# Expert rows scaled by their gates and added to token rows in DRAM by indirect transfers, in place of stores and gathers

## What is computed

```python
x = x + _L0_ffn_ref(_layernorm(x, axis=-1)[None], router_w, router_b, expert_w, expert_b)[0]
...
probs = jax.nn.softmax(logits, axis=-1)
top2_vals, top2_idx = jax.lax.top_k(probs, 2)
cw = cw.at[jnp.arange(n)[:, None], top2_idx].set(top2_vals)
h = jax.nn.gelu(jnp.einsum('nd,edh->neh', xf, W1) + b1[None], approximate=False)
y = jnp.einsum('neh,ehd->ned', h, W2) + b2[None]
out = jnp.einsum('ne,ned->nd', cw, y)
```

## Time and profile before

| | us |
|---|---|
| median of 3 runs (2142.50 to 2151.97) | 2149.12 |
| the profiled execution, its own time | 2141.64 |
| its span, first to last instruction | 2139.8 |
| TensorE matmuls busy | 1928.0 (90%) |
| VectorE busy | 757.1 (35%) |
| ScalarE busy | 397.3 (19%) |
| Pool busy | 132.0 (6%) |

### The profile page before, as it was taken

The page is one execution under the profiler, slowest core; times in us unless marked ns, Lnnn a source line. Parts: engine busy times, 40 slices in busy tenths (PEclk is TensorE's granted clock), DMA queues, the critical chain, the costliest instruction groups (busy, mean ns, idle before and its releaser), DMA issues.

```text
span 2139.8 us, 23079 instructions
## 1 busy us (share of the span) xinstructions
PE 1928.0 (90%) x7603; PEld 1234.0 (58%) x7604; DVE 757.1 (35%) x1715; ACT 397.3 (19%) x1046; POOL 132.0 (6%) x223
## 2 busy tenths in 40 slices
PE   5999999998999999779995999999999999399990
PEld 3555566566433446646663875555578589266560
DVE  3211322676688879411112511141111133311113
ACT  2331210024211112100100332000221211111110
POOL 0000000000000000011112300000000000111114
PEclk9999999999999999579997999999999999599995
DMA  6004000000000101424554410110010012434537
GB/s 174 0 1 155 2 0 1 19 1 0 20 29 28 42 21 44 162 74 176 188 180 131 139 59 0 44 45 0 0 45 1 0 59 61 159 125 170 183 118 223
DMA packets 58416, 154.05 MB, mean 72 GB/s; under 512 B 12574, under 2 KB 23218, under 8 KB 57893
## 3 DMA queue, kind: packets, MB, share of 16 engines
q1 hardware_dynamic: 34053, 87.05, 11.6%
q0 software_dynamic: 13200, 36.25, 5.5%
q10 hardware_dynamic: 11088, 29.77, 3.8%
HBM read 121.76 MB, written 34.78 MB: 73 GB/s over the span
## 4 chain that ended last, share of the span: by engine, by line
PE 86%; DMA 5%; DVE 4%; issue 2%; ACT 1%; DVEq 1%; POOL 1%; POOLq 0%; ACTq 0%; SPq 0%
PE PS L605 22%; PE PS L821 11%; PE PS L906 10%; PE PS L615 7%; PE PS L753 5%; PE PS L996 4%; PE PS L932 4%; PE PS L1016 4%; PE PS L669 4%; PE PS L973 3%; PE PS L959 3%; DMA WS<-in_fW 2%; DMA YG<-expert_rows,IDXA 2%; PE PS L884 1%; PE PS L803 1%
## 5 line engine op out<-in xcount | busy, mean ns | idle before, releaser
L605 PE MATMUL PS<-WS,XT 128*125 128x384 f32 x960 | 312.5, 487 | 1.4 <-issue 1.4
L821 PE MATMUL PS<-WR,F 125*65 125x500 f32 (+1 forms) x720 | 262.2, 518 | 2.5 <-DVE WR L1572 2.5
L605 PEld LDWEIGHTS PS<-WS,XT 128*125 128x125 f32 x960 | 180.0, 188 | 129.0 <-issue 2.6
L1572 DVE SCALAR_TENSOR_TENSOR WR<-RB,U,AT 125x500 f32<-125x500 f32 (+1 forms) x360 | 212.5, 647 | 22.0 <-PE PS L821 13.7
L906 PE MATMUL PS<-WS,XGT 128*128 x624 | 208.0, 490 | 0.0
L821 PEld LDWEIGHTS PS<-WR,F 125*65 125x65 f32 x720 | 97.6, 139 | 142.8 <-issue 99.8
L906 PEld LDWEIGHTS PS<-WS,XGT 128*128 128x128 f32 x624 | 117.7, 192 | 77.3 <-issue 2.5
L615 PE MATMUL PS<-XT,WS 128*128 128x416 f32 (+1 forms) x432 | 151.2, 512 | 0.0
L1698 DVE TENSOR_TENSOR YS<-PS,EBB 128x768 f32<-128x768 f32 x50 | 47.9, 958 | 270.5 <-PE PS L906 209.6
L615 PEld LDWEIGHTS PS<-XT,WS 128*128 128x128 f32 x432 | 81.6, 189 | 69.2 <-issue 69.2
L753 PE MATMUL PS<-OHS,OHD 125*125 125x418 bf16 x564 | 110.8, 351 | 0.0
(11 more groups left out here) (263 smaller groups left out, 1968.8 us busy)
## 6 DMA issues: line engine op xcount, KB each, us to landing
expert_rows<-YS ACTq DMA_DIRECT2D x50, 384.0 KB
WS<-in_ewT SPq DMA_DIRECT2D x8, 2304.0 KB, 10.6
WS<-in_fW SPq DMA_DIRECT2D x16, 1152.0 KB, 7.8
WS<-in_w SPq DMA_DIRECT2D x5, 2304.0 KB, 9.8
xn_rows<-XN ACTq DMA_DIRECT2D x20, 336.0 KB
RB<-expert_rows SPq DMA_DIRECT2D x12, 488.3 KB
WS<-in_wp SPq DMA_DIRECT2D x2, 2304.0 KB, 11.8
WS<-in_W SPq DMA_DIRECT2D x2, 2304.0 KB, 8.3
```

Of the source, the lines that this page charges most:

```text
L605: last = nc.tensor.matmul(ps[0:T, 0:HC], lhsT[:, k, t * T:(t + 1) * T], w[:, k, b * HC:(b + 1) * HC], start=(k == 0), stop=(k == KC - 1))
L821: last = nc.tensor.matmul(PS[0:DW, 2 * (u % 2) + j, 0:n], F[:, s, 2 * p + j, :], WR[:, k % WSLOTS, j, 0:n], start=(s == 0), stop=(s == NT ...
L1572: V.scalar_tensor_tensor(out=WR[:, k % WSLOTS, j, 0:nt * T], in0=RBS[u % RSLOTS][:, j, 0:nt * T], scalar=U[:, s, h:h + 1], in1=AT[:, s, t0 ...
```

## The change

The sum is kept in DRAM while the experts run. `X` is stored to the first 1250 rows of `y_d` behind routing (`keep_sums`). VectorE scales each block's rows by their gates, and Pool adds them to the tokens' rows in DRAM by an indirect transfer with an addition (`scatter`). The two rows of one token would otherwise be lost to each other if their transfers overlapped, so each scatter waits until the one before has landed. Padding rows are added to 128 spare rows behind the 1250. Behind stage one `X` is loaded back tile by tile; behind stage two the output is one copy from DRAM to DRAM. The store of each block on ScalarE's queue, the 20 gathers and the weighted sums of each stage are gone. To have each list place's gate and target row, routing gets one more round of 20 matmuls of 120 columns in bfloat16, with the gates split in three parts.

```diff
+        acc_d = y_d[0:N, :].rearrange("(t p) c -> p t c", p=T)
+
+        def keep_sums():
+            sp.dma_start(acc_d[0:PA], X[0:PA]).then_inc(acc_in, 16)
+            sp.dma_start(acc_d[PA:T], X[PA:T]).then_inc(acc_in, 16)
...
         sp.dma_start(EBB1, eb.partition_broadcast(P)).then_inc(eb_in, 16)
+        keep_sums()
         expert_loads(1, U_EW, U_MIX1)
 
         sp.wait_ge(experts_done, 1)
         load(U_MIX1)
+        sp.wait_ge(y_all, 1)
+        for t in range(NT):
+            sp.dma_start(X[0:PA, t, :], acc_d[0:PA, t, :]).then_inc(x_back[t], 16)
+            sp.dma_start(X[PA:T, t, :], acc_d[PA:T, t, :]).then_inc(x_back[t], 16)
...
         sp.dma_start(EBB3, fb2.partition_broadcast(P)).then_inc(eb_in, 16)
+        keep_sums()
         expert_loads(3, U_FF, len(units))
 
-        for t in range(NT):
-            sp.wait_ge(yg_used[3], summed(3, 2 * t + 1))
-            sp.dma_start(out[t * T:t * T + PA, :], X[0:PA, t, :]).then_inc(stored, 16)
-            sp.dma_start(out[t * T + PA:(t + 1) * T, :], X[PA:T, t, :]).then_inc(stored, 16)
-        sp.wait_ge(stored, 32 * NT)
+        sp.wait_ge(y_all, 2)
+        flat = (N * C) // 480
+        sp.dma_start(out.rearrange("n c -> (n c)").rearrange("(a b) -> a b", b=flat),
+                     y_d[0:N, :].rearrange("n c -> (n c)").rearrange("(a b) -> a b", b=flat)).then_inc(stored, 16)
...
+        def scatter(L, n, a, before):
+
+            pool.wait_ge(ys_ready[L], n + 1)
+            if not isinstance(before, int):
+                pool.wait_ge(ys_out[L][1 - a], before)
+            nc.gpsimd.tensor_tensor(SXF[:, a:a + 1], SIDX[:, bass.ds(n, 1)], ones[:, 0:1], ALU.mult)
+            pool.drain()
+            nc.gpsimd.tensor_copy(SX[:, a:a + 1], SXF[:, a:a + 1])
+            pool.drain()
+            nc.gpsimd.indirect_dma_start(out=y_d, out_offset=bass.IndirectOffsetOnAxis(ap=SX[:, a:a + 1], axis=0),
+                                         in_=YS[:, a, :], in_offset=None, compute_op=ALU.add).then_inc(ys_out[L][a], 16)
...
-            with nc.gpsimd.Fori(0, n) as i:
-                for a in range(2):
-                    b = (a + ahead) % 2
-
-                    pool.wait_ge(turned_n[L], i * 2 + a + ahead)
-                    gather(L, i * 2 + a + ahead, b)
-
+
+            def next_gather(i, a):
+                pool.wait_ge(turned_n[L], i * 2 + a + ahead)
+                gather(L, i * 2 + a + ahead, (a + ahead) % 2)
+
+            next_gather(0, 0)
+            next_gather(0, 1)
+            pool.wait_ge(gates_in, k)
+            pool.wait_ge(acc_in, 32 * k)
+            pool.wait_ge(y_cleared, 16)
+            scatter(L, 0, 0, 0)
+            with nc.gpsimd.Fori(1, n) as i:
+                next_gather(i, 0)
+                scatter(L, i * 2 - 1, 1, i * 16)
+                next_gather(i, 1)
+                scatter(L, i * 2, 0, i * 16)
+            scatter(L, n * 2 - 1, 1, n * 16)
             for b in range(2):
-                pool.wait_ge(ys_out[L][b], n * 16 + 16)
+                pool.wait_ge(ys_out[L][b], n * 16)
             nc.gpsimd.sem_inc(y_all, 1)
-            for q in range(KT):
-                if q >= YB[L]:
-                    pool.wait_ge(yg_used[L], summed(L, q - YB[L]))
-                nc.gpsimd.indirect_dma_start(out=YG[L][:, q % YB[L], :], out_offset=None, in_=y_d,
...
+            pe.wait_ge(gate_parts, k)
+            ps = begin(J.at[f"gates{L}"])
+            for q in range(KT):
+                last = nc.tensor.matmul(ps[:, 0:4 * ETC], OHR[:, q, :], TV2[:, q, :, :].rearrange("p a b -> p (a b)"),
+                                        start=(q == 0), stop=(q == KT - 1))
...
+            step(V.tensor_copy(GPB[:, 0], GW))
+            step(V.tensor_tensor(GR, GW, GPB[:, 0], ALU.subtract))
+            step(V.tensor_copy(GPB[:, 1], GR))
+            step(V.tensor_tensor(GR, GR, GPB[:, 1], ALU.subtract))
+            step(V.tensor_copy(GPB[:, 2], GR))
...
+                for m in range(3):
+                    V.tensor_tensor(tv[:, :, n, m, :], ot, GPB[:, m, n, :].unsqueeze(2).to_broadcast([T, NT, ETC]), ALU.mult)
+            V.tensor_copy(TV2[:, :, 3, :], OT)
...
             V.tensor_tensor(YS[:, a, :].rearrange("p (b c) -> p b c", b=2), PS[:, b0:b0 + 2, 0:HC],
                             EBB[L][:, bass.ds(e, 1), :].rearrange("p a (b c) -> p (a b) c", b=2), ALU.add).then_inc(y_free[L], 1)
+            V.drain()
+            V.tensor_scalar(YS[:, a, :], YS[:, a, :], GTE[:, bass.ds(n, 1)], None, ALU.mult).then_inc(ys_ready[L], 1)
...
         for t in range(NT):
-            weighted(1, t, 0)
-            V.drain()
-            weighted(1, t, 1)
+            dve.wait_ge(x_back[t], 32)
+            spread_of(2, t)
             if t:
                 normal(2, t - 1)
-            V.drain()
-            spread_of(2, t)
```

More of the change, by code:

```diff
@@ L50 @@
 QC = [(o, 250) for o in range(0, N, 250)]
[L51 removed]
+R_ROW0 = 1408
 class Jobs:
@@ L105, in plan_jobs @@
             j.add(f"tokens{L}", [v])
+            j.add(f"gates{L}", [v])
         else:
@@ L1200, in _ @@
         turns1 = nc.scalar.value_load(TAB[0:1, 2, 0:1], min_val=1, max_val=ET_MAX // 2)
-        act.wait_ge(y_cleared, 16)
         nc.scalar.drain().then_inc(y_free[1], 2)
         nc.scalar.drain().then_inc(xgt_ready[1], 1)
-        for b in range(2):
-            nc.scalar.drain().then_inc(ys_out[1][b], 16)
         columns_of(1, 0, 0)
@@ L1275, in _ @@
         nc.scalar.drain().then_inc(ht_ready[3], 1)
-        for b in range(2):
-            nc.scalar.drain().then_inc(ys_out[3][b], 16)
         def gelu(n, a):
@@ L1296, in _ @@
                 gelu(n + 1, 1 - a)
-                store(3, n, a)
     @block.vector
@@ L1691, in route @@
             V.drain().then_inc(tab_ready, 1)
+            step(V.tensor_copy(GPB[:, 0], GW))
[3 more added lines that the diff above has]
+            step(V.tensor_copy(GPB[:, 2], GR))
+            tv = TV2.rearrange("p (t k) v e -> p t k v e", k=2)
+            for n in range(2):
+                ot = OT.rearrange("p (t k) e -> p t k e", k=2)[:, :, n, :]
+                for m in range(3):
+                    V.tensor_tensor(tv[:, :, n, m, :], ot, GPB[:, m, n, :].unsqueeze(2).to_broadcast([T, NT, ETC]), ALU.mult)
+            V.tensor_copy(TV2[:, :, 3, :], OT)
+            V.drain().then_inc(gate_parts, 1)
+            ps = full(J.at[f"gates{L}"])
+            step(V.tensor_copy(GTE, ps[:, 0:ETC]))
+            step(V.tensor_tensor(GTE, GTE, ps[:, ETC:2 * ETC], ALU.add))
+            V.tensor_tensor(GTE, GTE, ps[:, 2 * ETC:3 * ETC], ALU.add)
+            step(V.tensor_scalar(SIDX, ps[:, 3 * ETC:4 * ETC], -1.0, 1.0, ALU.mult, ALU.add).then_inc(dve_emptied, 1))
+            V.tensor_scalar(TOKF[:, 0:1], pcol, float(N), None, ALU.add)
+            V.drain()
+            V.scalar_tensor_tensor(out=SIDX, in0=SIDX, scalar=TOKF[:, 0:1], in1=TOK, op0=ALU.mult, op1=ALU.add)
+            V.drain().then_inc(gates_in, 1)
         def expert_rows(L, n, a, i):
@@ L1696, in expert_rows @@
             dve.wait_ge(y_filled[L], n + 2)
[L1697 removed]
+            if not isinstance(i, int):
+                dve.wait_ge(ys_out[L][a], i * 16)
             V.tensor_tensor(YS[:, a, :].rearrange("p (b c) -> p b c", b=2), PS[:, b0:b0 + 2, 0:HC],
                             EBB[L][:, bass.ds(e, 1), :].rearrange("p a (b c) -> p (a b) c", b=2), ALU.add).then_inc(y_free[L], 1)
[L1701 to L1705 removed]
+            V.drain()
+            V.tensor_scalar(YS[:, a, :], YS[:, a, :], GTE[:, bass.ds(n, 1)], None, ALU.mult).then_inc(ys_ready[L], 1)
         V.drain()
@@ L1710, in _ @@
         turns1 = nc.vector.value_load(TAB[0:1, 2, 0:1], min_val=1, max_val=ET_MAX // 2)
-        with nc.vector.Fori(0, turns1) as i:
+        for a in range(2):
+            expert_rows(1, a, a, 0)
+        with nc.vector.Fori(1, turns1) as i:
             for a in range(2):
@@ L1817, in _ @@
         hidden_bias(0, 0)
-        with nc.vector.Fori(0, turns3) as i:
+        for a in range(2):
+            hidden_bias(a + 1, 1 - a)
+            expert_rows(3, a, a, 0)
+        with nc.vector.Fori(1, turns3) as i:
             for a in range(2):
@@ L1821, in _ @@
                 expert_rows(3, i * 2 + a, a, i)
-        weighted(3, 0, 0)
-        for t in range(NT):
-            if t + 1 < NT:
-                weighted(3, t + 1, 0)
-            V.drain()
-            weighted(3, t, 1)
-        V.drain().then_inc(done, 1)
     block_ctx.__exit__(None, None, None)
```

61 lines of the change are left out of this document (22 added, 39 removed).

## The result

The changed kernel takes 2319.1 us (median of four runs, 2313.2 to 2321.0) against 2150.4 for the kernel before beside it: a ratio of 1.080, interval 1.078 to 1.083. It is slower, as forecast, and by 169 us where 97 was forecast. The profiled execution has a span of 2317.1 us, 177.3 more than before.

The account below looks back on a forecast made before the run. Pool, held through both indirect transfers, was to bound the kernel at 11.5 us a block. Stage one +78.5, behind it -9.3, stage two +57.4, behind it -29.3 make +97.3 on 2149.1: 2246.5 us, range 2190 to 2370.

Parts of the forecast that it names:

- the hold of Pool: At Pool's drains behind each indirect issue: Pool is held until the transfer in flight has landed; chance 0.52.
- six places: Six gathers at the two stages' starts with another gather behind them, each with 2.7 to 3.0 us idle on Pool.
- held until its issue is written: Pool held only for the issue, 4.95 us for gather and scatter alike; 10.4 us a block, 2195 us; chance 0.13.
- the scatter's slot: Pool's time per scatter in a block: 5.5 until landed + 0.1 + 0.95 to the next issue = 6.55 us.
- not held: Pool isn't held at all behind an indirect issue; 9.1 us a block, 2132 us; chance 0.10.
- The scatter's price: Landing time of one block's scatter-add into DRAM: 5.5 us, the middle between 4.9 and 6.2.
- The start and both ends: Stage one starts 1.6 us later, stage two 0.3; behind stage one 20.8 us (-9.3), behind stage two 22.0 (-29.3).
- The period: Time per block in both expert stages: 11.5 us, set by Pool, against 8.4 of TensorE.
- Pool's own sum: Pool's time per block for its two indirect transfers: gather 4.95 + scatter 6.55 = 11.5 us.
- the ring: Two-block round of landed gather, TensorE block, vector work, Pool, scatter, next gather; 20.75 or 18.2 us in two rivals.
- The clock rival: TensorE's clock falls in the idle gaps, 3.4 us more a block; 12.9 us a block, 2315 us; chance 0.10.
- the dearest scatter: Upper price of the scatter-add, a gather and then a store: 6.2 us, giving 2280 us.

Follow-up runs that it names:

- e10: e5 with one bare drain of Pool in front of each of the two issues of a block; 2302.0 us (one run).
- e5: Changed kernel with VectorE writing both index columns; Pool's loop only waits and issues, with no small operation or drain; 2187.6 us, ratio 1.021 to the kernel before.
- e4: Changed kernel loading only a sixth or less of the weights of experts 2 to 7 in both stages; 2295.9 us, ratio 1.071 to the kernel before.
- e1: Changed kernel with each gather issued one place earlier in Pool's order; 2285.2 us, ratio 1.066 to the kernel before.
- e8: e5 and e1 joined, with VectorE waiting for the gather whose index column it overwrites; 2115.1 us, ratio 0.986 to the kernel before.
- e2: Changed kernel with 18 filler products of the identity on TensorE behind each block's products; 2306.9 us, ratio 1.076 to the kernel before.
- e6: Changed kernel with nine filler products of the identity on TensorE behind each block's products; 2311.3 us (one run).
- e3: Changed kernel with a plain scatter that doesn't add, so the sums are left out; 2285.8 us, ratio 1.066 to the kernel before.

## Why the prediction was right, and where its size was wrong

**What bounds, and the hold of Pool: right.** Idle time ahead of Pool's casts behind every indirect issue, TensorE waiting for the gathered rows, and spacing far above 8.4 were all there. That the hold lasts until landing was an inference from six places; e10 now shows it at 73 (a drain ends within 0.1 us of the landing), and e5 and e10 together show that the drain does it. The rival "held until its issue is written" wanted the same 4.95 for gather and scatter; the scatter's slot of 6.5 to 6.8 rules it out. The rule of the Trainium skill, DMA: Bandwidth & Descriptors, "Anatomy of one DMA — SWDGE (gpsimd) path", by which most of a transfer's fixed time is not the issuing engine's, was weighed against this for the rival "not held". Both hold: in e5 the engine issues again 1.89 us behind a scatter, and only the drain makes it wait for the rest.

**The scatter's price: right.** 5.5 forecast, 5.6 measured; slot 6.55 forecast, 6.5 to 6.8 measured. The gather's landing is the 3.9 of before.

**The start and both ends: right within 5 us.** The first bias addition of stage one stands at 936.2, where 940.6 was forecast for the block's end, and all of this execution before routing runs 4.5 us ahead of the old one. Behind stage one, 1289.10 - 1264.85 = 24.3 us (20.8 forecast, 30.1 before); behind stage two, 23.2 (22.0 forecast, 51.3 before): the output copy landed in 13.7 us (12.4 forecast). The store of X stayed hidden: the first scatter of each stage is issued 1.5 us behind its rows, as forecast.

**The period: the step that failed.** The forecast named blocks 11 to 12 us apart as its sign; they are 13.35 apart. It took Pool's own sum, 4.95 + 6.55 = 11.5, as the period, and kept the ring (landed, block, vector work, Pool, scatter, gather) for the rivals. It gave TensorE 3.1 us of idle time in every block and took each block at full clock. With the forecast's own terms the ring at full clock is (8.4 + 2.0 + 1.5 + 6.55 + 3.9) / 2 = 11.2, only 0.3 below the sum. Anything that lengthens it by more than 0.6 us a round makes it the bound, and two things did:

- The clock. Blocks behind a wait run at the lower of the two levels: the window from 1069.6 to 1073.6 has 0.52, the transposes take 1.54 instead of 0.66, and the products behind them 8.9 to 10.4 instead of 7.9. With that and the slot of 6.8, a round without weights beside it (gather 4.0, block 10.7, vector 2.2, Pool 1.4, slot 6.8) is 25.1 us, or 12.55 a block; e4 measures 12.7. The clock rival had this mechanism, with 3.4 us a round, where 10.7 - 8.4 = 2.3 is measured, and so 12.9. It was given 0.10 and held to be an alternative to the forecast. It is a consequence of it: whoever forecasts 3 us of idle time a block must forecast the clock too.
- The weights. A gather beside a load of weights lands in up to 7.6 us; e4 takes 0.65 a block of this away. The forecast took the median of the earlier trace rows for all 50 gathers, although its longest of 7.9 stood beside it.

Sorted by the ladder, the 1.85 us are 0.65 weights, 0.8 clock and 0.4 the scatter's slot and Pool's rest (11.9 against 11.5), times 44 = 81 us. That the total of 2315 in the clock rival comes close to the measured time is luck in part: its clock term is too large by about half and it has none for the weights. That 2319 lies in the range of 2190 to 2370 is owed to the room that the range left for rivals; the forecast's own sum ends at 2246.5, or 2280 with the dearest scatter.

## What to carry over

- On Pool, keep index arithmetic and its drains away from indirect transfers: let another engine write the index column, and let Pool only wait and issue. Here that was worth 130 of 2319 us with the same transfers.
- Where an engine issues two kinds of transfers in turn, write the ring through all waits beside the engine's own sum, also when the sum is the larger: two bounds 0.3 us apart are one bound, and small delays fall on the ring. Issuing the gather one place ahead of the wait for rows opens it (e1, e8).
- A forecast wait of several us on TensorE carries its clock with it. A filler that tests this must end just before the awaited transfer lands: the longer one took the place of the wait (e2), and the shorter one left waits behind which the clock fell (e6).

## What the runs showed of the hardware

- A drain on Pool with an indirect transfer in flight ends when that transfer has landed: 4.7 us from a gather's issue to the next, 6.3 from a scatter-add's, against 1.9 without a drain (e10, e5). In 73 cases of e10 it ended 0.07 to 0.08 us behind the landing, whether that took 3.7 or 7.7 us.
- A scatter-add of 128 rows of 768 f32 into DRAM lands in 5.6 us and takes Pool 1.60 us to issue; a plain scatter of the same rows lands in 3.1 and takes 1.01 to 1.03 (e3); a gather lands in 3.9 and takes 0.98 to 1.01. A gather that is issued 1.9 us behind a scatter-add lands in 5.2 (e5).
- Pool's multiply directly behind a scatter-add's issue takes 0.74 to 0.77 us (0.19 where nothing is in flight); behind a plain scatter it takes 0.20 to 0.21.
